# Loads of up to six tiles in a ring of 24, with fewer buffers for 0.0 and 1.0, weight parts and counts

## The reference, cut to what matters

```python
embs = [jnp.dot(x, w) for x, w in zip(xs, ws)]
emb_sum = sum(embs)                                   # written as a loop
q_emb = sum(jnp.dot(x ** 2, w ** 2) for x, w in zip(xs, ws))
fm_ans = 0.5 * (emb_sum ** 2 - q_emb)
return jnp.concatenate([fm_ans] + embs, axis=-1)      # 1024 x 704, float32
```

## Time and profile before

| | before |
|---|---|
| median of 3 runs | 278.85 us |
| the profiled execution | 278.5 us, of it 276.7 us span |
| busy: PE, VectorE, ScalarE, GpSimd | 215.7, 225.0, 225.4, 110.9 us |
| moved by DMA | 113.85 MB, mean 412 GB/s |
| x loads | 72, of 256 KB to 2 MB |
| granted TensorE clock, mean | 0.975 |

### The profile page before, as it was taken

One profiled execution on the slowest core, in us unless ns is written; L12 is line 12 of the kernel. 1 busy time (PEld: TensorE's weight loads), 2 busy tenths in 40 slices (PEclk: granted clock), 3 DMA queues, 4 the chain that ended last, 5 costly groups with the idle time before them and its releaser, 6 DMA issues.

```text
span 276.7 us, 2763 instructions
## 1 busy us (share of the span) xinstructions
PE 215.7 (78%) x892; PEld 153.8 (56%) x892; DVE 225.0 (81%) x150; ACT 225.4 (81%) x280; POOL 110.9 (40%) x78
## 2 busy tenths in 40 slices
PE   0439988799988867969787787778778788689994
PEld 0326756577666545646554555555555565466753
DVE  3677967788799788968978988987987997999885
ACT  0758799999988688979878878877877886899983
POOL 0446665966324109356334134044044041083800
PEclk9975799999999999999999999999999999999999
DMA  7999999999999999999999999999999999999996
GB/s 233 418 394 423 413 438 423 421 422 418 426 430 422 418 420 410 427 421 436 420 429 427 420 431 421 426 421 427 416 429 433 421 420 424 406 416 410 410 395 246
DMA packets 17374, 113.85 MB, mean 412 GB/s; under 512 B 3168, under 2 KB 4448, under 8 KB 11216
## 3 DMA queue, kind: packets, MB, share of 16 engines
q1 hardware_dynamic: 11936, 106.89, 92.7%
q10 hardware_dynamic: 5424, 6.79, 6.8%
HBM read 110.79 MB, written 2.88 MB: 411 GB/s over the span
## 4 chain that ended last, share of the span: by engine, by line
DMA 68%; issue 13%; PE 8%; ACT 8%; DVE 1%; ACTq 1%; SPq 0%
DMA x_ring<-in_x_dram 63%; PE sums L507 7%; ACT is_set L396 6%; DMA whole<-in_w_dram 5%; PE sums L514 1%; ACT whole L386 1%; ACT turned L408 1%; DVE is_one L590 1%; ACTq L373 1%; ACT results L413 0%; DVE total L610 0%; DVE results L633 0%; ACTq L380 0%; ACTq L381 0%; PE sums L552 0%
## 5 line engine op out<-in xcount | busy, mean ns | idle before, releaser
L590 DVE TENSOR_SCALAR_CACHE_REDUCE is_one<-x_ring 128x4096 uint8<-128x4096 f32 (+4 forms) x67 | 221.4, 3320 | 46.5 <-DMA x_ring<-in_x_dram 45.2
L396 ACT ACTIVATE is_set<-x_ring 128x2048 fp32r<-128x2048 uint32 (+2 forms) x112 | 192.2, 1719 | 31.8 <-DMA x_ring<-in_x_dram 31.1
L507 PE MATMUL sums<-is_set,low 128*128 128x512 f32 x398 | 134.7, 419 | 57.3 <-ACT is_set L396 51.7
L507 PE MATMUL sums<-is_set,high 128*128 128x512 f32 x398 | 126.9, 400 | 0.0
L507 PEld LDWEIGHTS sums<-is_set,low 128*128 128x128 f32 x398 | 69.6, 193 | 97.0 <-ACT is_set L396 43.8
L507 PEld LDWEIGHTS sums<-is_set,high 128*128 128x128 f32 x398 | 76.7, 193 | 17.5
L477 POOL CAST high<-whole 128x1024 fp32r<-128x1024 f32 (+5 forms) x31 | 27.0, 872 | 146.6 <-ACT whole L386 146.6
L479 POOL TENSOR_TENSOR low<-whole,high 128x1024 fp32r<-128x1024 f32 (+5 forms) x31 | 60.8, 1961 | 2.5
L396 ACT ACTIVATION_READ_ACCUMULATOR is_set<-x_ring 128x1 f32 (+1 forms) x112 | 21.1, 189 | 0.0
L386 ACT ACTIVATE whole<-whole 128x512 f32<-128x512 f32 (+5 forms) x31 | 16.6, 536 | 4.2 <-DMA whole<-in_w_dram 4.2
L485 POOL TENSOR_TENSOR total<-total,turned 128x1024 f32<-128x1024 f32 x8 | 19.2, 2395 | 0.0
(11 more groups left out here) (29 smaller groups left out, 6.8 us busy)
## 6 DMA issues: line engine op xcount, KB each, us to landing
x_ring<-in_x_dram SPq DMA_DIRECT2D x39, 2048.0 KB, 21.0
x_ring<-in_x_dram SPq DMA_DIRECT2D x19, 512.0 KB, 17.9
x_ring<-in_x_dram SPq DMA_DIRECT2D x6, 1024.0 KB, 21.3
whole<-in_w_dram ACTq DMA_DIRECT2D x19, 256.0 KB, 9.9
x_ring<-in_x_dram SPq DMA_DIRECT2D x3, 1536.0 KB, 21.7
out_dram<-results SPq DMA_DIRECT2D x9, 256.0 KB, 9.3
x_ring<-in_x_dram SPq DMA_DIRECT2D x4, 256.0 KB, 13.8
x_ring<-in_x_dram SPq DMA_DIRECT2D x1, 448.0 KB, 6.3
```

The lines of the kernel that those rows point to most:

```text
L396: nc.scalar.activation(is_set[chunk.k % SETS][0:chunk.rows, 0:length], in_ring(chunk.place, length)[0:chunk.rows].bitcast(U32), ACT.Sign, ...
L507: last = nc.tensor.matmul(sums[:, summing(n, half), :], w, x[0:chunk.rows, at:at + HALF], start=first, stop=False, skip_group_check=True)
L590: nc.vector.tensor_scalar(is_one[c % 2][0:rows, 0:length], in_ring(at, length)[0:rows], 1.0, None, ALU.is_equal, ALU.add, accum_out=one_co ...
```

## The change

- `LOAD` goes from 4 to 6 and `RING` from 20 to 24. `plan_counts` joins chunks across the groups of a table, and holds to 4 tiles from chunk 80 on (18 chunks ahead of the last table). There are then 61 loads in 55 counts: 21 loads have 6 tiles (rows of 24 KB). The loads of the last table keep their sizes.
- `SETS` goes from 5 to 4: ScalarE's chunk k waits for PE's chunk k-4 to be over where it waited for k-5.
- `PAIRS` goes from 4 to 3: GpSimd waits for group g-3 where it waited for g-4.
- `is_one` is one buffer of 6 KB instead of two of 4 KB, and each count waits for the count just before it.
- Table 9's single tile is loaded as 128 rows instead of 112, and the code for fewer rows goes (also in the general path, which does not run here).

```diff
-TAIL = [-(-(v - P * (tiles - 1)) // 16) * 16 for v, tiles in zip(VOCABS, TILES)]
+TAIL = [-(-(v - P * (tiles - 1)) // 16) * 16 if tiles > 1 else P for v, tiles in zip(VOCABS, TILES)]
...
-LOAD = 4
-RING = 20
+LOAD = 6
+RING = 24
 LANDS = 16
-SETS = 5
+SETS = 4
 WHOLES = 3
-PAIRS = 4
+PAIRS = 3
 AHEAD = 3
...
-    for group in GROUPS:
+    for place in range(NT):
         joined = []
-        for chunk in group.chunks:
-            most = 2 if group.table == LAST else LOAD
+        for chunk in CHUNKS[BEGIN[place]:END[place]]:
+            group = chunk.group
+            most = 2 if group.table == LAST else 4 if chunk.k > BEGIN[NT - 1] - 18 else LOAD
             if joined and (chunk.tail and group.table != LAST or len(chunk.halves) == 1
                            or sum(c.n for c in joined) + chunk.n > most):
                 lists.append(joined)
...
-        is_one = [sb(f"is_one{i}", [P, LOAD * BATCH], U8) for i in range(2)]
+        is_one = sb("is_one", [P, LOAD * BATCH], U8)
...
-            def count_ones(at, length, rows, c):
-                if c >= 2:
-                    dve.wait_ge(ones_counted, c - 1)
+            def count_ones(at, length, c):
+                if c:
+                    dve.wait_ge(ones_counted, c)
                 nc.vector.tensor_scalar(
-                    is_one[c % 2][0:rows, 0:length], in_ring(at, length)[0:rows], 1.0, None,
-                    ALU.is_equal, ALU.add, accum_out=one_counts[0:rows, c:c + 1]
-                    ).then_inc(ones_counted, 1)
+                    is_one[:, 0:length], in_ring(at, length), 1.0, None, ALU.is_equal, ALU.add,
+                    accum_out=one_counts[:, c:c + 1]).then_inc(ones_counted, 1)
```

More of the change, by code:

```diff
@@ L69, in __init__ @@
         self.tail = tile + n == TILES[table]
-        self.rows = TAIL[table] if TILES[table] == 1 else P
         self.group = self.count = None
 class Load:
-    def __init__(self, i, table, tile, n, first, width, rows, at):
-        self.i, self.table, self.tile, self.n, self.rows, self.at = i, table, tile, n, rows, at
+    def __init__(self, i, table, tile, n, first, width, at):
+        self.i, self.table, self.tile, self.n, self.at = i, table, tile, n, at
         self.first, self.width, self.length = first, width, n * width
@@ L89, in __init__ @@
         self.c, self.loads, self.chunks = c, loads, chunks
-        self.at, self.length, self.rows = loads[0].at, sum(load.length for load in loads), loads[0].rows
+        self.at, self.length = loads[0].at, sum(load.length for load in loads)
         for chunk in chunks:
@@ L132 @@
 NGROUPS, NCHUNKS = len(GROUPS), len(CHUNKS)
+BEGIN = [min(g.chunks[0].k for g in GROUPS if g.place == n) for n in range(NT)]
+END = [max(g.end for g in GROUPS if g.place == n) for n in range(NT)]
 def plan_counts():
     lists = []
-    for group in GROUPS:
+    for place in range(NT):
         joined = []
-        for chunk in group.chunks:
-            most = 2 if group.table == LAST else LOAD
+        for chunk in CHUNKS[BEGIN[place]:END[place]]:
+            group = chunk.group
+            most = 2 if group.table == LAST else 4 if chunk.k > BEGIN[NT - 1] - 18 else LOAD
             if joined and (chunk.tail and group.table != LAST or len(chunk.halves) == 1
@@ L162, in plan_counts @@
         for tile, n in parts:
-            own.append(Load(len(loads) + len(own), one.table, tile, n, one.first, one.width, one.rows, at))
+            own.append(Load(len(loads) + len(own), one.table, tile, n, one.first, one.width, at))
             at += own[-1].length
@@ L183 @@
 NCOUNTS = len(COUNTS)
-G_ORDER = [9] + [t for t in range(NT) if t != 9]
-BEGIN = [min(g.chunks[0].k for g in GROUPS if g.place == n) for n in range(NT)]
-END = [max(g.end for g in GROUPS if g.place == n) for n in range(NT)]
 W_LOADS = [sum(other.loads for other in GROUPS[:group.g + 1] if other.whole == group.whole)
@@ L321, in _ @@
                 at = load.tile * BATCH + load.first
-                sp.dma_start(in_ring(load.at, load.length)[0:load.rows],
+                sp.dma_start(in_ring(load.at, load.length),
                              x_end[load.table][:, load.first:load.first + load.width] if load.tail else
@@ L337, in _ @@
                 base = zeros = 0
-                for t in G_ORDER:
+                for t in range(NT):
                     end, rows = TILES[t] - 1, TAIL[t]
@@ L348, in _ @@
                     sp.wait_ge(g_multiplied, base + end + 1)
-                    sp.dma_start(in_ring(0, BATCH)[0:x_end[t].shape[0]], x_end[t]).then_inc(gx_landed, 16)
+                    sp.dma_start(in_ring(0, BATCH), x_end[t]).then_inc(gx_landed, 16)
                     w_end, before = w_dram[t][:, end * D:TILES[t] * D], P - rows if end else 0
@@ L396, in count_set @@
                 nc.scalar.activation(
-                    is_set[chunk.k % SETS][0:chunk.rows, 0:length],
-                    in_ring(chunk.place, length)[0:chunk.rows].bitcast(U32), ACT.Sign,
-                    accum_out=set_counts[0:chunk.rows, chunk.k:chunk.k + 1]).then_inc(set_counted, 1)
+                    is_set[chunk.k % SETS][:, 0:length], in_ring(chunk.place, length).bitcast(U32),
+                    ACT.Sign, accum_out=set_counts[:, chunk.k:chunk.k + 1]).then_inc(set_counted, 1)
             def copy_sums(n):
@@ L502, in multiply @@
                     for part in (low, high):
-                        w = part[group.pair][0:chunk.rows, chunk.at + t, :]
+                        w = part[group.pair][:, chunk.at + t, :]
                         first = chunk.k == BEGIN[n] and t == 0 and part is low
@@ L507, in multiply @@
                             last = nc.tensor.matmul(sums[:, summing(n, half), :], w,
-                                                    x[0:chunk.rows, at:at + HALF], start=first,
-                                                    stop=False, skip_group_check=True)
+                                                    x[:, at:at + HALF], start=first, stop=False,
+                                                    skip_group_check=True)
                 last.then_inc(x_multiplied, 1)
@@ L601, in _ @@
                     dve.wait_ge(x_landed[load.land], 16 * (load.turn + 1))
-                count_ones(count.at, count.length, count.rows, count.c)
+                count_ones(count.at, count.length, count.c)
             n = NT - 1
@@ L628, in _ @@
             part = final.length // 2
-            count_ones(final.at, part, final.rows, NCOUNTS - 1)
+            count_ones(final.at, part, NCOUNTS - 1)
             for half, blocks in enumerate(halves):
@@ L635, in _ @@
                                                op0=ALU.mult, op1=ALU.subtract).then_inc(fm_ready, 1)
-            count_ones(final.at + part, part, final.rows, NCOUNTS)
+            count_ones(final.at + part, part, NCOUNTS)
             dve.wait_ge(flag_ready, 1)
@@ L649, in _ @@
                 dve.wait_ge(stored, 16 * (NT + 2))
-                g_link(nc.vector.memset(in_ring(0, BATCH), 0.0))
                 nc.vector.nop().then_inc(g_multiplied, 1)
```

## The result

The changed kernel takes 279.63 us (median of 7 runs, 279.43 to 279.79); the kernel before, on the same chip, 278.72 us (7 runs, 278.56 to 278.89). The ratio is 1.0029 [1.002, 1.0039]: 0.9 us slower, where 0.67 us less was forecast, and just outside the range. The profiled execution took 279.78 us, of it 277.9 us span (before: 278.5 and 276.7).

What follows compares the result with a forecast made beforehand. The prediction took the full DMA queue as the bound, with packets priced beside bytes. Profiled 278.5 - 0.83 + 0.16 = 277.8 us; as a median, 278.85 - 0.67 = 278.2 us, range 277.6 to 279.6.

Steps and rivals of the forecast that it cites:

- Fewer loads, 0.83 us: x loads on the DMA queue: 72 become 61, 1584 packets less at 8.4 ns over 16 engines, saving 0.83 us.
- a and b: DMA engine time per packet, 8.4 ns, and per MB, 36.87 us, solved from two full windows of the kernel before.
- the fit: Two full DMA windows, mostly 16 KB and 4 KB packets, solved for a price of 8.4 ns a packet.
- the rival of cut rows: x loads: rows of 24 KB are cut in two, 2688 more packets, 1.41 us, giving 279.6 us; chance 0.07.
- the gain is not there: x loads: packets of 16 KB already run as fast as any, so 0 + 0.16 us, 279.0 us; chance 0.21.
- Behind that stands a chain that does not change: Kernel end, from last chunk (268.40) to last store issued (273.62): unchanged, so the 0.83 us saved is on the path.
- a changed tail after the last landing: Kernel end, behind the last x load: listed among the signs that the forecast is wrong, with no size.
- Table 9 with 128 rows, +0.16 us: Load of table 9's tile: 16 more rows of 4 KB cost 0.15 us for bytes and 0.01 us for packets.
- Ring and queue never dry, 0: SP's x loads, ring of 24 in steps of 6: each issued before the queue runs dry, 7 us in hand early; cost 0.
- SETS, PAIRS and one `is_one`, 0: Waits on fewer buffers in ScalarE, GpSimd and VectorE: hidden by the full queue; bounds up to 1.9 and 0.1 us, taken as 0.
- Late weights: Weight loads wait behind longer packets, landing after 14.5 to 16 us; counted at 0, or 283 us if queue starves, chance 0.12.
- the point from which it decides: Weight landing time, about 17 us, from which ScalarE's waits delay x loads; at 20 us the queue is dry some 5 us.

Runs made afterwards that it cites:

- small buffers: Kernel before with SETS 4, PAIRS 3, one is_one and 128 rows for table 9, loads of 4 and ring of 20 kept: 278.04 us, 0.998 of before.

## Why the prediction was wrong, point by point

**Fewer loads, 0.83 us: right in size.** Packets to the count (15808 in all against 15806, the two more being the tail's fetches; q1 exact). Loads of six against four bring 0.7 to 0.8 us in whole runs and 0.7 in the last chunk. The two windows of after do not confirm a and b, since their error is as large as the effect, but the packets themselves show a price of that order: x packets of 16 KB take a median of 616 ns, of 24 KB 918 ns, so 48 KB in two packets instead of three takes 1836 instead of 1848 ns, 12 ns for a packet saved where the fit said 8.4. In after the last chunk is only 0.81 us earlier instead of 1.2 with the rows' 0.5; that 0.4 us is open. Rows of 24 KB are one packet each, so the rival of cut rows is out, and so is "the gain is not there".

**"Behind that stands a chain that does not change": the step that failed.** It was followed for data and not for code. From the last chunk to the flag it holds (5.77 us after, 5.79 before). Behind the flag it does not: 11 counts fewer took 21 instructions out of VectorE's program (32 by the trace's records) and moved its branch to where the target must be fetched: 2.2 us more for the step, 2.0 us more for the kernel. The prediction named "a changed tail after the last landing" as what would make it wrong, but gave it neither a price nor a chance. The trace of before could have warned, though not given the price: the last instruction of work is at 274.2 us and the end at 276.7, and VectorE's step over the general path ends only 0.3 us ahead of SP's, which sets the end. That its 0.6 us holds for one position only took the runs to see.

**Table 9 with 128 rows, +0.16 us: wrong in sign.** It gives 0.5 to 0.8 us back. The step priced bytes at the rate of full windows; the small load did not run at that rate before (288 GB/s), and a window on it, 6:8, would have shown it. Rows and loads together are 1.2 us by the traces, of which 0.4 is missing in after, and the branch takes 2.0: hence 1.2 more in the span, 0.9 in the median.

**Ring and queue never dry, 0: right.** No slice of DMA is under 9 between the first and the last, and with loads of six moving the weights earlier brings nothing.

**SETS, PAIRS and one `is_one`, 0: right to 0.1 us** by spans (small buffers 276.1, 128 rows alone 276.2; 0.2 us by the ratios). One wait of GpSimd for PE of 8.1 us appears in after with 24 idle instructions and costs nothing.

**Late weights: the mechanism right, the point from which it decides not.** The loads issued in 36:43 and 46:52 landed after 15.6 and 16.3 us (14.5 to 16 was forecast; 9.7 and 10.6 before). The squares that waited for them in after:

```profile
45.93 0.64 ACT L385 ACTIVATE whole<-whole 128x512 f32<-128x512 f32 x1 [1.65 <-DMA whole<-in_w_dram]
...
54.64 0.63 ACT L385 ACTIVATE whole<-whole 128x512 f32<-128x512 f32 x1 [3.62 <-DMA whole<-in_w_dram]
...
62.47 0.63 ACT L385 ACTIVATE whole<-whole 128x512 f32<-128x512 f32 x1 [0.61 <-DMA whole<-in_w_dram]
```

```profile
ACT whole L385 <- DMA whole<-in_w_dram: 15.2, 8, 4.0
```

That is 5.9 us by 63 us (8 by 60 was forecast, 3 to 8 as a sign of being right) and 15.2 in the whole run against 4.2 before; the later waits were in no forecast. The stated point from which it decides, a landing of about 17 us, is not borne out: with loads of eight the queue ran dry behind a landing of 13.7 us, and loads of six lost nothing at 16.3. It depends as much on how many loads the ring holds.

## What to carry to other kernels

A sum of data movement ends at the last data; what stands behind it is code, and a taken branch over a long block that is not run is part of it. Look at the step from that branch to its target on every engine, and at which engine is last, and where a change alters the number of instructions ahead of it, give the tail a range of some 2 us; when two versions are compared, try one of them with a few idle instructions, since a gain of 0.5% was hidden here by 8 missing ones. Price a small odd-sized load by its own window, not by the rate of the full ones.

## What the runs showed of the hardware

- VectorE's branch over 171 or 172 instructions: 0.6 us, or 2.8 to 3.1 us with two fetches of 8 KB, by its place in the code alone.
- VectorE's code was fetched in packets of 8 KB, one for some 128 of its records.
- An x packet of 4, 8, 16, 24 and 32 KB took a median of 161, 315, 616, 918 and 1219 ns.
- A load of 112 partitions moved 288 GB/s with engines shown as full, one of 128 partitions 404.
- Small packets wait behind long ones: a weight load of 256 KB landed, in the steady stage 130:200, in a median of 9.8 us beside x rows of 16 KB and 12.3 us beside rows of 24 KB.
- While ScalarE waited for weights, PE idled, and the granted clock then fell to its lower level (1.2 GHz) for some us. PE stood still for 4.7 us up to 57.3, and the clock is 0.70 in 56:60 below, 0.50 in 58:60; the mean is 0.941 against 0.975. No cost of it shows: with 8 idle instructions the mean is 0.946, and that kernel has the whole gain. Window of after, columns as for 6:8:

```profile
56.00:60.00 4.00, 2.74 (x7) 2.23 (x8) 2.48 (x2) 4.00 (x6) 2.75 (x2) 0.70 1.03 434
```
